# Choosing PSUM banks by the slot in which each is expected free, in a two-layer cross-attention kernel on one core

## The reference

```python
q, k_text, v_text = x @ Wq, text @ Wk, text @ Wv          # text: 77 rows (layer 0), 252 (layer 1)
probs    = softmax(q_h @ k_h.T * scale)                    # per head
text_out = probs @ v_h
text_probs = softmax(q @ k_text.T * scale)                 # all heads together, layer 0
sem      = (text_probs @ text) @ ip.T * scale
ip_probs = softmax(q_h @ ip_k_h.T * scale + 0.5 * sem) * spatial_mask
out      = (text_out + ip_probs @ ip_v_h) @ Wout + bias + x
```

## Time and profile before

| what | us |
|---|---|
| time of the kernel, median of 3 runs | 1695.24 (1691.83 to 1708.3) |
| the profiled execution's own time | 1690.93 |
| its span | 1689.1 |
| TensorE matmul busy (PE) | 1616.2, 96% of the span |
| weight loads (PEld) | 1434.5, 85% |
| VectorE (DVE) | 1350.9, 80% |
| ScalarE (ACT) | 1032.3, 61% |
| GpSimd (POOL) | 848.1, 50% |
| chain that ended last | TensorE 79%, VectorE 8%, ScalarE 5% |

### The profile page before, as it was taken

How to read it: one execution, slowest core, us unless ns; L and a number is a source line. 1 busy time by engine, 2 the same in 40 slices (tenths; PEclk the granted TensorE clock), 3 DMA queues, 4 the chain that set the end, 5 groups by cost and what they waited for, 6 DMA issues and landing times.

```text
span 1689.1 us, 42966 instructions
## 1 busy us (share of the span) xinstructions
PE 1616.2 (96%) x14568; PEld 1434.5 (85%) x14568; DVE 1350.9 (80%) x3617; ACT 1032.3 (61%) x2204; POOL 848.1 (50%) x789
## 2 busy tenths in 40 slices
PE   6999999999999999998999999999999999999986
PEld 5888888888888888878888888898989888888966
DVE  4677777777777777877788988898888888998884
ACT  3566656656666566656666666666666666666652
POOL 3223422222222222334777676677667766776562
PEclk9999999999999999999999999999999999999998
DMA  8333443343333333542333322332233223332201
GB/s 220 103 102 111 122 125 116 117 122 113 118 117 118 114 116 117 154 128 88 98 95 91 96 82 82 99 104 80 75 99 108 84 67 99 110 87 55 86 30 42
DMA packets 185985, 172.72 MB, mean 102 GB/s; under 512 B 25760, under 2 KB 185770, under 8 KB 185770
## 3 DMA queue, kind: packets, MB, share of 16 engines
q1 hardware_dynamic: 185770, 169.98, 34.6%
HBM read 110.17 MB, written 57.76 MB: 99 GB/s over the span
## 4 chain that ended last, share of the span: by engine, by line
PE 79%; DVE 8%; ACT 5%; issue 4%; SPq 2%; POOL 1%; DMA 1%; DVEq 0%; POOLq 0%; ACTq 0%
PE MISC L103 25%; PE GP L103 17%; PE NAT L232 9%; PE TR L262 7%; PE PV L309 5%; PE PV L293 4%; PE PV L290 2%; PE PV L312 2%; PE MISC L341 2%; DVE TA L807 1%; PE MISC L484 1%; ACT PH L537 1%; DVE PM L820 1%; PE PV L250 1%; ACT PVS L544 1%
## 5 line engine op out<-in xcount | busy, mean ns | idle before, releaser
L984 POOL TENSOR_TENSOR ZS<-ZP 128x256 f32<-128x256 f32 x267 | 263.6, 988 | 219.5 <-DVE ZP L814 219.2
L530 ACT ACTIVATE P<-TA 128x512 f32<-128x512 f32 x320 | 202.0, 631 | 264.8 <-DVE TA L807 264.4
L232 PE MATMUL NAT<-KS,QS 65*128 65x256 f32 x1280 | 293.8, 311 | 4.3 <-DMA KS<-qk_parts 3.2
L262 PE MATMUL TR<-QS,KS 69*128 69x256 f32 (+1 forms) x1280 | 270.4, 293 | 0.3 <-DVE TA L807 0.2
L215 POOL TENSOR_TENSOR PARTS<-QKF,PARTS 112x508 fp32r<-112x508 f32 (+3 forms) x93 | 122.8, 1320 | 277.2 <-ACT PARTS L558 276.1
L814 DVE TENSOR_TENSOR ZP<-GP,PM 128x512 f32<-128x512 f32 x320 | 219.0, 684 | 51.2 <-PE GP L103 40.8
L103 PE MATMUL GP<-PH,GH 128*128 128x256 f32 (+1 forms) x960 | 244.0, 284 | 16.3 <-DVE ZP L814 16.3
L232 PEld LDWEIGHTS NAT<-KS,QS 65*128 65x128 f32 x1280 | 201.8, 190 | 67.7 <-issue 62.0
L798 DVE TENSOR_REDUCE MX<-NAT 128x2 f32<-128x504 f32 x320 | 215.4, 673 | 36.4 <-PE NAT L232 33.7
L103 PE MATMUL GP<-PH,GL 128*128 128x256 f32 (+1 forms) x960 | 240.9, 279 | 0.0
L820 DVE SCALAR_TENSOR_TENSOR PM<-P,PH 128x512 f32<-128x512 f32 x320 | 233.6, 730 | 0.9 <-ACT PH L537 0.9
(11 more groups left out here) (278 smaller groups left out, 3952.0 us busy)
## 6 DMA issues: line engine op xcount, KB each, us to landing
QS<-qk_parts SPq DMA_DIRECT2D x480, 64.0 KB
KS<-qk_parts SPq DMA_DIRECT2D x480, 64.0 KB
qk_parts<-PARTS SPq DMA_DIRECT2D x128, 224.0 KB, 2.8
CT<-in_ctx_t SPq DMA_DIRECT2D x32, 512.0 KB, 4.3
qk_parts<-PARTS SPq DMA_DIRECT2D x64, 192.0 KB, 2.4
QS<-NH SPq DMA_DIRECT2D x480, 4.0 KB
XT<-in_x_t SPq DMA_DIRECT2D x48, 112.0 KB, 2.3
XT<-x_t SPq DMA_DIRECT2D x48, 112.0 KB, 2.4
```

The costliest lines, as they stand in the source:

```text
L232: ins = e.matmul(NAT[s % 2][:, i * T:(i + 1) * T], QS[0:KQ, h, i * 128:(i + 1) * 128], KS[0:KQ, h, :], start=True, stop=True)
L262: ins = e.matmul(TR[s % 2][:, i * S:(i + 1) * S], KS[0:w, h, i * 128:(i + 1) * 128], QS[0:w, h, :], start=True, stop=True)
L530: e.activation(P[:, s % NP, :], TA[:, s % 2, :], ACT.Exp, scale=SCALE).then_inc(q["exp"], 1)
L984: e.tensor_tensor(ZS[s % NZ][:, :], ZP[:, s % 2, 0:S], ZP[:, s % 2, S:2 * S], ALU.add).then_inc(q["zs"], 1)
```

## The change

1. **Banks.** `Ring.take` no longer picks the bank taken longest ago, but the one with the smallest `until`, a number that each taker gives: its own slot plus the number of slots after which the bank should be free (1.3 by default in layer 0, 0.8 in layer 1; others by item). The wait itself stays on the same semaphores.
2. **"on"** (transposes of `PVS`) moves to the front of a slot, ahead of NAT: in layer 0 from the middle of slot `HG + 3` to the front of slot `HG + 4`, in layer 1 within slot `HG + 5`. ScalarE's copy of it moves to the front of the slot too.
3. **"hst"** of layer 0 moves from slot 8 to the front of slot 9, and `HTL` from slot 9 to 10; **"sem"** from the end of slot 6 to its front, with ScalarE's copies `SN` and `ST`.
4. **"yt"** moves from slots 10 and 11 to 12 and 13, the store behind it by one slot, **"ptt"** of layer 1 from slot 13 to 12.

No instruction is added or taken away.

```diff
-AT0 = dict(... hst=48, htl=49, om=(64, 67), y=(65, 68), yt=(70, 71), out=69, out_t=73)
+AT0 = dict(... hst=49, htl=50, om=(64, 67), y=(65, 68), yt=(72, 73), out=69, out_t=74)
-           ptt=73, hst=(74, 76), htl=(75, 77), om=(78, 82), y=(79, 83), out=84, xb_in=66)
+           ptt=72, hst=(74, 76), htl=(75, 77), om=(78, 82), y=(79, 83), out=84, xb_in=66)
...
-    def take(self, key, freed, among=3):
-        n = min(range(among), key=lambda i: self.age[i])
-        free, self.freed[n], self.age[n] = self.freed[n], freed, self.clock
-        self.clock += 1
+    def take(self, key, freed, until, among):
+        n = min(range(among), key=lambda i: self.until[i])
+        free, self.freed[n], self.until[n] = self.freed[n], freed, until
...
-    def take(key, freed, t):
-        return ring.take(key, freed, 3 if t < S1 - 2 else 2)
+    def take(key, freed, t, slots=None):
+
+        return ring.take(key, freed, t + (slots or (1.3 if t < S1 else 0.8)), 3 if t < S1 - 2 else 2)
...
         for t in range(T0, T1):
+            for off, lo, hi, width in ((HG + 4, 0, G1, 4), (HG + 5, G1, 2 * G1, 2)):
+                g = due_group(t, off, lo, hi)
+                if g is not None:
+                    k, free = take(("on", g), (q["on"], g + 1), t, 0.5)
+                    e.wait_ge(*free)
+                    e.wait_ge(q["pvs"], g + 1)
...
+            b = of0(t, AT0["hst"])
+            if b is not None:
+                for i in range(2):
+                    k, free = take(("hst", b, i), (q["ht_lo"], 2 * b + i + 1), t, 1.5 + 0.2 * i)
...
+            b = of0(t, AT0["sem"])
+            if b is not None:
+                k, free = take(("sn", b), (q["sn"], b + 1), t, 0.6)
...
+                k, free = take(("st", b), (q["st"], b + 1), t, 0.9)
...
-                    k, free = take(("om", b, i), (q["y"], 2 * b + i + 1), t)
+                    k, free = take(("om", b, i), (q["y"], 2 * b + i + 1), t, 1.4)
...
-                    k, free = take(("qk", b, m), (q["qk_hi"], 3 * b + m + 1), t)
+                    k, free = take(("qk", b, m), (q["qk_hi"], 3 * b + m + 1), t, 2.3 if b < B else 1.8)
```

More of the change, by code:

```diff
@@ L350, in _ @@
                 ins.then_inc(q["ptt"], 1)
[L351 to L360, removed]
             for i, off in enumerate(AT1["hst"]):
@@ L363, in _ @@
                 if b is not None:
-                    k, free = take(("hst", B + b, i), (q["ht_lo"], 2 * (B + b) + i + 1), t)
+                    k, free = take(("hst", B + b, i), (q["ht_lo"], 2 * (B + b) + i + 1), t, 1.4)
                     e.wait_ge(*free)
@@ L431, in _ @@
                 ins.then_inc(q["tpt"], 1)
[L432 to L438, removed]
-                    ins = e.matmul(k[:, i * NI0:(i + 1) * NI0], TPT[:, i * 128:(i + 1) * 128], G0[:, NT0:T], start=True, stop=True)
-                ins.then_inc(q["snm"], 1)
-                k, free = take(("st", b), (q["st"], b + 1), t)
-                e.wait_ge(*free)
-                for i in range(2):
-                    ins = e.matmul(k[:, i * S:(i + 1) * S], G0[:, i * 128:(i + 1) * 128], TPT[:, :], start=True, stop=True)
-                ins.then_inc(q["stm"], 1)
             for n, off in enumerate(AT0["v"]):
@@ L512, in _ @@
         for t in range(T0, T1):
+            g = due_group(t, HG + 4, 0, G1)
+            if g is not None:
+                b, hg = divmod(g, NGRP)
+                if b >= 2 and hg == 0:
+                    e.wait_ge(q["hs"], b - 1)
+                e.wait_ge(q["ont"], g + 1)
+                e.copy(ON0[:, b % 2, :, :, :].rearrange("p v a (h s) -> p (v a) h s", s=NV0)[:, :, HG * hg:HG * hg + HG, :],
+                       ring.bank["on", g][:, :].rearrange("p (v h s) -> p v h s", v=4, s=SLOT)[:, :, :, 0:NV0]).then_inc(q["on"], 1)
+            g = due_group(t, HG + 5, G1)
+            if g is not None:
+                b, hg = divmod(g - G1, NGRP)
+                if g == G1:
+                    e.wait_ge(q["hs"], B)
+                if b >= 2 and hg == 0:
+                    e.wait_ge(q["tx"], b - 1)
+                e.wait_ge(q["ont"], g + 1)
+                e.copy(heads_of(b)[:, :, HG * hg:HG * hg + HG, :],
+                       ring.bank["on", g][:, 0:256].rearrange("p (v h s) -> p v h s", v=2, s=SLOT)[:, :, :, 0:NV]).then_inc(q["on"], 1)
+            b = of0(t, AT0["hst"])
+            if b is not None:
+                for i in range(2):
+                    if b:
+                        e.wait_ge(q["om"], 2 * (b - 1) + i + 1)
+                    e.wait_ge(q["hst"], 2 * b + i + 1)
+                    e.copy(HT[0][0:CK, :, i * 128:(i + 1) * 128],
+                           ring.bank["hst", b, i][0:CK, 0:384].rearrange("p (c q) -> p c q", c=3)).then_inc(q["ht_hi"], 1)
+            b = of0(t, AT0["sem"])
+            if b is not None:
+                if b >= 2:
+                    e.wait_ge(q["mx"], H * (b - 1))
+                    e.wait_ge(q["sum"], H * (b - 1))
+                e.wait_ge(q["snm"], b + 1)
+                e.copy(SN[:, b % 2, :, :], ring.bank["sn", b][:, 0:2 * NI0].rearrange("p (a t) -> p a t", a=2)).then_inc(q["sn"], 1)
+                e.wait_ge(q["stm"], b + 1)
+                e.copy(ST[:, b % 2, :], ring.bank["st", b][:, :]).then_inc(q["st"], 1)
             g = due_group(t, HG - LEAD + 1)
@@ L591, in _ @@
             for i in range(2):
-                for b in both(t, AT0["hst"], AT1["hst"][i]):
+                b = of1(t, AT1["hst"][i])
+                if b is not None:
+                    b += B
                     if b:
@@ L652, in _ @@
                 e.copy(TPT[:, :], ring.bank["tpt", b][0:NT0, 0:S]).then_inc(q["tpts"], 1)
-            b = of0(t, AT0["sem"])
-            if b is not None:
-                if b >= 2:
-                    e.wait_ge(q["mx"], H * (b - 1))
-                    e.wait_ge(q["sum"], H * (b - 1))
-                e.wait_ge(q["snm"], b + 1)
-                e.copy(SN[:, b % 2, :, :], ring.bank["sn", b][:, 0:2 * NI0].rearrange("p (a t) -> p a t", a=2)).then_inc(q["sn"], 1)
-                e.wait_ge(q["stm"], b + 1)
-                e.copy(ST[:, b % 2, :], ring.bank["st", b][:, :]).then_inc(q["st"], 1)
             for n, off in enumerate(AT0["v"]):
```

56 lines of the change are left out of this document (24 added, 32 removed).

## The result

The changed kernel takes 1690.25 us (median of 11 runs, 1682.11 to 1695.62), the kernel before 1699.04 (11 runs of the same comparison, 1690.21 to 1708.30). The ratio is 0.9943, with a 95% interval from 0.9918 to 0.9969: 0.6% faster. The interval doesn't reach 1, but the gain is under the 1% that the forecast took for the least that can be told, and the time is 16 us above the 1674 of the forecast. In experiments 9 and 11 one run each took far longer than the rest (1990.11 and 3146.69 us, for no cause that the records show); the ratios leave them out.

A forecast was written before the change was run, and what follows sets the result against it. TensorE was taken to set the pace in both layers. Gains of 13.0 (layer 0) and 7.8 (layer 1), 20.8 us, off the profiled 1690.93 gave 1670.1; with 4.3 for the median, 1674 us, range 1661 to 1691.

The forecast's parts named there:

- parts 1 and 3: Waits removed: in layer 0's slots 11 and 7, 1.03 and 0.27 us per batch; in layer 1's slot 13, 0.60.
- The 1.30: Layer 0, slots 11 and 7: total waiting that the change removes per batch, 1.03 + 0.27 us.
- part 2: Layer 0, slot 10: the new order makes "v" wait 0.29 us per batch for HTL, bounds nothing to 1.7.
- 5.40 + 0.82 = 6.22: Layer 0, VectorE from slot 6's maxima to HTL: four MX with TA take 5.40 us, NH and the addition 0.82.
- Rival B: Layer 0: VectorE's chain is at its slow upper end, "v" waits 1.7 us per batch; 1692 us in all; chance 0.07.
- instead of 1.0: Layer 0: net gain per batch in us, 1.30 removed less 0.3 of new waiting at "v".
- Rival D: Layer 1, slot 12: "ptt" waits 2.4 us per batch for VectorE's FU; slower, 1705 us; chance 0.05.
- 20.8: Whole kernel: total gain in us, 13.0 from layer 0 and 7.8 from layer 1, over 13 batches each.
- with 3 us either way: Passage between the layers and tail: left as they are in the sum, allowed 3 us either way.
- a longer passage: Between 720 and 900 us: a longer passage was listed as a sign that the forecast is wrong; no size given.
- The 4.3 us: Whole kernel before: the median of its runs lies 4.3 us above the profiled execution, so this was added to 1670.1.
- C: Both layers: bubbles only move to a bank one slot later; gain some 8 us, 1687; chance 0.20.

The follow-up runs named there:

- experiment 9: The changed kernel with "hst" of layer 0's last batch one slot earlier, "ptt" in slot 13, NAT made 2 to 4 times in few passage slots: 1682.58 us.
- Experiment 11: The changed kernel with the semantic products "sem" and their copies left at the end of slot 6: 1693.40 us.
- experiment 5: The kernel before, unchanged, timed and profiled again as a kernel of its own: 1699.52 us.
- experiment 2: The changed kernel with the old bank rule, the bank taken longest ago: 1691.07 us.
- experiment 4: The changed kernel with each NAT product of slots 312 to 344 made twice: 1689.14 us.
- experiment 6: The changed kernel with NAT made twice in slots 306 to 344 and TR three times in slots 318 to 344: 1702.67 us.
- experiment 7: The changed kernel with layer 0's "hst" back at the front of slot 8 and HTL in slot 9: 1692.43 us.
- experiment 1: The kernel before with the new bank rule and its numbers, every item at its old place: 1727.41 us.
- experiment 3: The changed kernel with "hst" and its low part one slot earlier in layer 0's last batch: 1688.23 us.
- experiment 10: The kernel before with the same added NAT products as experiment 9: 1698.28 us.
- experiment 12: The kernel of experiment 9 without its repeated NAT products: 1687.28 us.
- experiment 8: The changed kernel with "ptt" of layer 1 back in slot 13: 1687.54 us.

## Why the prediction was right or wrong

**Slots 7, 11 and 13 (parts 1 and 3).** Right in the main. The waits for NH, for `SN` and for the copy of "on" are gone. The 1.30 was some 0.1 too high: a transpose takes 0.11, not 0.10 (the six of "hst" take 0.58 because the next matmul starts 0.03 behind the last of them). The sum of start-to-start distances by tile, per steady batch of layer 0, shows both sides (us, the time from the start of such a matmul to the start of the next, before and after):

```
TR                   6.54  5.88   -0.66   0.90 of waiting before "on" gone, 0.23 before "v" come
"on" (IDENT,PVS)     2.36  1.78   -0.57
query projection     1.32  1.06   -0.26
"yt" (IDENT,XB)      0.69  0.54   -0.15
"om"                 0.99  0.89   -0.11
"hst" (IDENT,HS)     0.58  0.95   +0.37
NAT, keys, sem       (four rows, together +0.49)
net                               -0.89
```

**The new wait at "v" (part 2).** There, 0.23 us where 0.29 was forecast. TensorE after the change:

```profile
336.74 0.27 PE L238 MATMUL MISC<-IDENT,HS 128*112 128x128 f32 x1
337.18 0.54 PE L238 MATMUL MISC<-IDENT,HS 128*112 128x128 f32 x3 [0.17 <-DVE XB L789]
...
340.04 0.48 PE L296 MATMUL TR<-QS,KS 69*128 69x256 f32 x2
340.58 0.37 PE L103 MATMUL MISC<-WVH,CTSH 128*77 128x320 f32 x1
```

And before:

```profile
340.80 0.49 PE L262 MATMUL TR<-QS,KS 69*128 69x256 f32 x2
```

Before, this pair of TR, behind the transposes of the maxima, took 341.12 - 340.80 = 0.32. After, "v" comes 340.58 - 340.04 = 0.54 behind it, so it waits 0.22 (0.23 in the table) for HTL. No row of waits names it, because the record of TR is still open. VectorE ran at the short distance:

```profile
333.61 0.32 DVE L801 TENSOR_REDUCE MX<-NAT 128x2 f32<-128x154 f32 x1 [1.42 <-PE NAT L266]
...
336.65 0.47 DVE L789 TENSOR_TENSOR XB<-MISC,XB 128x320 f32<-128x320 f32 x1
337.05 0.30 DVE L801 TENSOR_REDUCE MX<-NAT 128x2 f32<-128x154 f32 x1
...
338.40 0.30 DVE L801 TENSOR_REDUCE MX<-NAT 128x2 f32<-128x154 f32 x1
...
339.15 0.67 DVE L818 TENSOR_TENSOR TA<-TR,ST 128x512 f32<-128x512 f32 x1
339.97 1.02 DVE L781 TENSOR_TENSOR HTL<-MISC,HTH 112x384 fp32r<-112x384 f32 x2
340.91 0.31 DVE L801 TENSOR_REDUCE MX<-NAT 128x2 f32<-128x154 f32 x1
```

One slot's maxima and sum take 338.40 - 337.05 = 1.35, the distance that the forecast used, and the maxima behind HTL start at 340.91, 0.08 ahead of the end of its record (339.97 + 1.02). From slot 6's maxima to HTL it is 339.97 - 333.61 = 6.36, where the forecast added up 5.40 + 0.82 = 6.22. Rival B, with 1.65 per slot, is out. With it goes the literal reading of the drain rule (the Trainium skill, VectorE: DVE Perf Modes, The DRAIN you can't avoid), that an operation starts only when the pipe of the one before is empty: the trace disagrees with that reading by 0.30 us per slot. The same section adds that an operation which is not held starts earlier.

**A wait that was missed.** In the rows above, the second half of "hst" starts 0.44 after the last transpose of the first half (337.18 - 336.74), where 0.11 is the distance: 0.33 per batch for the addition `XB` (336.65 + 0.47 = 337.12), which frees the bank of "om" that the second half of "hst" takes. Part 2 named this addition as work in VectorE's queue, but never asked who waits for it. Together VectorE holds TensorE up for 0.33 + 0.23 = 0.56 per batch where 0.29 was forecast; that the second part alone is near 0.29 is luck, since TensorE comes to "v" later by the first. Experiment 11 ties both to "sem" at the front: with "sem" at the end the first is gone and the second 0.13. Against them stand 0.26 us at the query projection which had not been seen either. The misses nearly cancel: 0.89 instead of 1.0.

**Layer 1.** 0.62 measured, 0.60 forecast; the size is right and the reason in the main. "ptt" was said to cost nothing, and it doesn't, but it brings nothing either (55.21 without, 55.27 with). Rival D is out: no wait for FU in the steady part. The bank rule, which gives the change its name, is worth 0.2 of the 0.62, and nothing in layer 0.

**The sum.** The steady parts give 12 x 0.89 + 13 x 0.62 = 18.7 where 20.8 was forecast. What failed is the sentence "The passage between the layers and the tail I leave as they are, with 3 us either way." The passage is 10.8 us longer, the start and the first two batches 2.7, the tail 4.2. The prediction had named a longer passage as a sign of being wrong. Of the passage's 10.8, some 9 are the clock: the same kernel before lost 12 us there when it had 27.3 us at half clock (experiment 5), and the changed one has 20.4. About 1 is the collision of "hst" with the query projections. Of the 2.7 at the start 2.0 are in batch 0, where the changed kernel's profile has 3.4 us at half clock from 75.5 us on; four other profiles with the new places and without such a stretch there (experiments 2, 4, 6 and 7) take 41.1 to 41.2 for this batch instead of 42.7, so some 1.6 are the clock. The tail goes by the clock too, as the profiles of all kernels show together:

| at half clock in the rest (behind batch 30) | length of the rest | profiles |
|---|---|---|
| 10.2 | 81.0 | before |
| 13.6 to 14.2 | 82.4 to 82.6 | experiments 1, 2, 3, 5, 6, 7, 9, 10, 12 |
| 17.0 | 83.8 | 11 |
| 20.4 | 84.6 to 85.2 | the changed kernel, 4, 8 |

Both orders are in the second row, so the tail's 4.2 are nearly all clock. Together that is some 15 of the 17.7 us lost. The sum had no term for the clock: it was made on a profile with 1.00 granted throughout the passage.

**The baseline.** The forecast was set against one profiled execution, and that had before's most favourable clock, 0.995, which it has in a quarter of its runs (23 of 92). The 4.3 us that the text added for the median didn't mend that, since none of the changed kernel's runs reaches this clock. Against a profile of before at nearly the changed kernel's own clock (experiment 5, 0.986 against 0.985, span 1703.0) the changed kernel's 1688.5 is 14.5 us less.

**Rivals B and C** gave 1692 and 1687, nearest to the 1690.25 measured, but by mechanisms that didn't happen. B's slow VectorE chain is answered above. C had the bubbles only move, and in the steady parts they went. C was right for experiment 1 alone, where the bank rule without the new places exchanged the waits for worse ones. The words of the Trainium skill that stood behind it (Perfetto Trace Analysis, Optimization Strategy) say that such bubbles can mean too little PSUM; it wasn't so here, since most of them went with the same three banks.

**What stays open.** Why the clock falls near 750 us in every profile with the new places. TensorE's stretch ahead of the fall, of the kernel after:

```profile
748.29 0.50 PE L266 MATMUL NAT<-KS,QS 65*128 65x256 f32 x2 [0.85 <-DVE MX L809]
748.98 0.47 PE L296 MATMUL TR<-QS,KS 69*128 69x256 f32 x2 [0.18 <-DVE TA L818]
749.89 0.47 PE L266 MATMUL NAT<-KS,QS 65*128 65x256 f32 x2 [0.44 <-DVE MX L809]
...
751.69 1.95 PE L327 MATMUL PV<-P,VB 128*32 128x256 f32 x16
753.57 2.75 PE L485 MATMUL GP<-KBD,QKF 112*128 112x28 f32 x12
```

And of the kernel before, the same work:

```profile
756.46 0.50 PE L232 MATMUL NAT<-KS,QS 65*128 65x256 f32 x2 [0.56 <-DVE MX L798]
757.14 0.47 PE L262 MATMUL TR<-QS,KS 69*128 69x256 f32 x2 [0.19 <-DVE TA L807]
758.05 0.47 PE L232 MATMUL NAT<-KS,QS 65*128 65x256 f32 x2 [0.44 <-DVE MX L798]
...
759.68 1.05 PE L293 MATMUL PV<-P,VB 128*32 128x256 f32 x16
760.66 1.52 PE L484 MATMUL GP<-KBD,QKF 112*128 112x28 f32 x12
```

The order is the same, and the wait for the maxima 0.3 longer in the kernel after. Then the same 16 products take 1.95 instead of 1.05 and "scm" 2.75 instead of 1.52: the clock fell at 751.3. In experiment 5, which has the order of before, it fell at 761.0, just ahead of the same 16 products, which take 1.93 there. So this place is fragile in both orders, and every one of the ten profiles with the new places has half clock from 748 to 754 us on. Feeding it didn't cure it: the stretch there is 3.4 us long in experiment 4, 20.5 in 6 and 17.1 in 9, against 10.2 to 17.1 in those without a feed. A better pairing of the two layers' items in slots 310 to 316 wasn't tried.

## What to carry to other kernels

Before a profile is made the base of a sum, compare its granted clock with the clocks of the other runs: here one hundredth of it is 14 us, as much as the whole change. A gain per batch in the steady part says nothing of the passages, where the same change shifts what meets what; forecast them by themselves. And for every bank that an item newly takes, ask which copy frees it: the one that wasn't asked about costs 0.33 us per batch here, against a gain of 0.89.

## What the runs showed that was not expected

- The clock of an almost fully busy TensorE still falls. In experiment 8 TensorE is busy for all of 40 us, at full clock, and 4 us later is granted half:

```profile
1104.00:1107.00 3.00, 3.00 (x16) 3.00 (x14) 1.43 (x3) 2.48 (x5) 0.47 (x1) 0.50 0.00 0
1060.00:1100.00 40.00, 40.00 (x376) 36.20 (x375) 35.91 (x65) 26.95 (x59) 28.50 (x30) 1.00 0.35 102
```

- Each such stretch of 3.4 us costs 1.6: three batches of that kernel take 56.77 instead of 55.20.
- The clock of whole runs comes in groups. The kernel before is at 0.995 in 23 of its 92 runs, at 0.993 in 6, never at 0.991, 0.992 or 0.994, and at 0.990 or less in 63; the first group is 6.5 us faster than the runs at 0.990, so a median of few runs can fall on either side.
- Making TensorE busier is no sure cure: the medians are 4.7 us lower with the feed of experiment 9 than without (not shown to be its doing), the same with that of 10, and some 12 us higher than the changed kernel's with that of 6.
